# First group's mixer sums, statistics and norm factors placed among the last scan steps

## The reference

```python
# mixer (Mamba), 256 channels x 16 states, scanned over time
def step(h, inp):
    a, b, c = inp
    h = a * h + b
    y = (h * c[:, None, :]).sum(-1)
    return (h, y)
y = ys.transpose(1, 0, 2) + xm * Dp
y = y * silu(z)
x = x + y @ w_out                      # "mixed rows"
h = layernorm(x, ln2_g, ln2_b)         # statistics and factors of the mixed rows
h = gelu(h @ w_ff1 + b_ff1) @ w_ff2 + b_ff2
return x + h                           # and the caller adds this to its own x once more
```

## Time and profile before

| | |
|---|---|
| median of three runs | 940.75 us (940.24 to 942.75) |
| the profiled execution, time | 941.38 us |
| its span in the trace | 939.5 us, 13919 instructions |
| PE busy | 643.7 us (69%) |
| DVE busy | 711.1 us (76%) |
| ACT busy | 538.4 us (57%) |
| POOL busy | 449.6 us (48%) |
| scan instructions `L1232`, 128 of them | 290.5 us busy, 2270 ns each |
| `L1595` matmuls, 1024 of them | 133.6 us busy, 274 ns each |

### The profile page before, as it was taken

How to read it: one execution, slowest core, us unless ns; L and a number is a source line. 1 busy time by engine, 2 the same in 40 slices (tenths; PEclk the granted TensorE clock), 3 DMA queues, 4 the chain that set the end, 5 groups by cost and what they waited for, 6 DMA issues and landing times.

```text
span 939.5 us, 13919 instructions
## 1 busy us (share of the span) xinstructions
PE 643.7 (69%) x4284; PEld 513.3 (55%) x4285; DVE 711.1 (76%) x1785; ACT 538.4 (57%) x1116; POOL 449.6 (48%) x301
## 2 busy tenths in 40 slices
PE   4996116874898767778787887778799971159600
PEld 3775006862343367677676776677677760058600
DVE  6877883446754689999999999999988757845311
ACT  1562002232667989999999999999654620013200
POOL 3000005637400059898989899898710000047474
PEclk9998556996999869999999999999999995559955
DMA  8001101332100123332333233333500002014333
GB/s 203 7 1 53 38 0 43 100 76 54 36 1 6 28 57 104 102 100 101 101 100 104 97 104 95 100 101 101 169 1 1 1 26 64 0 31 109 80 97 81
DMA packets 61778, 62.79 MB, mean 67 GB/s; under 512 B 9079, under 2 KB 42682, under 8 KB 61722
## 3 DMA queue, kind: packets, MB, share of 16 engines
q1 hardware_dynamic: 57178, 52.77, 19.3%
q0 software_dynamic: 4544, 9.32, 4.6%
HBM read 50.40 MB, written 11.67 MB: 66 GB/s over the span
## 4 chain that ended last, share of the span: by engine, by line
DVE 31%; ACT 26%; PE 21%; POOL 11%; issue 8%; DMA 3%; DVEq 0%; POOLq 0%; SPq 0%; ACTq 0%
ACT work L775 12%; DVE work L1232 12%; POOL work L567 6%; POOL r_zs L572 5%; ACT wfold L747 4%; DVE work L985 4%; ACT dBuT L747 4%; PE bank L1678 3%; DMA work<-normed_rows,source 2%; PE bank L1666 1%; PE decay_ps L1666 1%; PE bank L1457 1%; PE decay_ps L1468 1%; PE decay_ps L1625 1%; PE decay_ps L1546 1%
## 5 line engine op out<-in xcount | busy, mean ns | idle before, releaser
L1232 DVE TENSOR_TENSOR_SCAN work<-work,decay_ps 128x1024 f32<-128x1024 f32 x128 | 290.5, 2270 | 1.9 <-PE decay_ps L1582 1.9
L583 POOL TENSOR_TENSOR work<-work,C_bc 128x1024 f32<-128x1024 f32 x86 | 204.5, 2378 | 110.2 <-DVE work L1232 109.7
L567 POOL DMA_INDIRECT work<-normed_rows,source x78 | 74.9, 961 | 297.0 <-DVE source L1085 271.9
L775 ACT ACTIVATE work<-r_delta,Aneg 128x510 f32<-128x510 f32 x256 | 170.1, 712 | 9.0 <-DVE work L1232 7.5
L1595 PE MATMUL bank<-ident,work 128*128 128x128 f32 x1024 | 133.6, 274 | 0.1
L1595 PEld LDWEIGHTS bank<-ident,work 128*128 128x128 f32 x1024 | 116.7, 142 | 0.3 <-POOL work L583 0.3
L583 POOL TENSOR_TENSOR work<-work,win_s 128x1024 f32<-128x1024 f32 x42 | 99.9, 2378 | 11.0 <-DVE work L1232 11.0
L1582 PE MATMUL decay_ps<-ident,wfold 128*128 128x128 f32 x512 | 70.5, 282 | 37.4 <-DVE wfold L1224 24.5
L1582 PE MATMUL decay_ps<-ident,dBuT 128*128 128x128 f32 x512 | 69.5, 280 | 34.5 <-DVE dBuT L1224 34.5
L1582 PEld LDWEIGHTS decay_ps<-ident,wfold 128*128 128x128 f32 x512 | 56.8, 144 | 50.1 <-ACT wfold L747 41.7
L747 ACT ACTIVATE wfold<-duT,B_T 128x256 f32<-128x256 f32 x192 | 82.8, 494 | 1.4 <-PE decay_ps L1582 1.4
(11 more groups left out here) (262 smaller groups left out, 1268.6 us busy)
## 6 DMA issues: line engine op xcount, KB each, us to landing
C_bc<-routed_out SPq DMA_DIRECT2D x86, 256.0 KB, 3.1
win_s<-routed_out SPq DMA_DIRECT2D x42, 256.0 KB, 3.1
routed_out<-work SPq DMA_DIRECT2D x26, 192.0 KB
normed_rows<-r_zs SPq DMA_DIRECT2D x2, 2048.0 KB, 9.4
X<-in_L_attn_a_input_data SPq DMA_DIRECT2D x4, 512.0 KB, 5.7
r_du<-in_L_ffn_W SPq DMA_DIRECT2D x2, 1024.0 KB, 6.7
r_du<-in_L_ffn_W SPq DMA_DIRECT2D x4, 512.0 KB, 8.3
out<-X SPq DMA_DIRECT2D x8, 256.0 KB, 2.4
```

Of the source, the lines that this page charges most:

```text
L567: pool.indirect_dma_start(out=xin[:, i % 2, s, :], out_offset=None, in_=normed_rows, in_offset=bass.IndirectOffsetOnAxis(ap=source[:, k:k ...
L583: pool.tensor_tensor(h[:, m % 4], h[:, m % 4], col(C_bc[m % 3]).broadcast_to([P, NB, G]), ALU.mult).then_inc(c_hC, 1)
L775: last = A(o, d, ACT.Exp, scale=Aneg[:, b, n:n + 1])
L1232: V.tensor_tensor_scan(h[:, m % 4].rearrange("p b t -> p (b t)"), decay[:, m % 2].rearrange("p b t -> p (b t)"), decay_ps[:, m % 2].rearra ...
```

## The change

- out_proj(0) moves to PE's step m = 112 of the scan loop and writes bank 3 instead of bank 4; y_of(6, 0), the next user of bank 3, waits for p_xa of group 0.
- DVE computes XA of group 0 behind scan(113), its statistics behind scan(114), and the 18 factor instructions in scan steps 115 to 122: two links a step, one directly behind the scan and one behind scaled_last (and gated); the first link holds three instructions. The last one is followed by a wait for its own end and the increment of d_factors.
- X is no longer updated by four instructions a group from PSUM (`L1268`), but by one that adds XA over all four tiles (`twice_mixed`). The set-up of `gate` as 1 + rs goes.
- DVE after the loop: mixed(1), twice_mixed(0), factors_of(1), gated(7, 0), mixed(2), factors_of(2), gated(7, 1), finished(0), as before from there.
- PE after turned_dBu(127): summed(124), summed(125), out_proj(1), mixed_turned(0), summed(126), hidden(0) chunks 0 and 1, summed(127), chunks 2 and 3, out_proj(2), y_of(7, 0), mixed_turned(1), dense_out(0), y_of(7, 1), out_proj(3), hidden(1), ... Chunk 3 of group 0 goes to bank 2 instead of bank 1 and waits for chunk 0's gelu.
- ACT after the table load: mixed_rows(0) (waits for scan 126), mixed_turned(0), gelu of chunks 0 and 1, turned_y(7), gelu of chunks 2 and 3, mixed_rows(1), mixed_turned(1), mixed_rows(2), ...

```diff
+def hidden_bank(g, c):
+    return HIDDEN_BANK[0 if g == 0 and c == FFC - 1 else c]
 def slot(i, kind):
...
 GATES = (4, 6)
+FIRST_LINK = STEPS - N + 3
+LAST_LINK = 15
 FIRST = 1
...
     act.preload_act_table(ACT.Gelu_apprx_tanh)
-    act.wait_ge(c_dBu, STEPS)
-    turned_y(NG - 1)
     f = ffn[1]
...
         for c in range(FFC):
+            if g == 0 and c == 0:
+                act.wait_ge(c_y, STEPS - 1)
+            if g == 0 and c == 2:
+                act.wait_ge(c_dBu, STEPS)
+                turned_y(NG - 1)
             act.wait_ge(d_h_ps, g * FFC + (c + 1))
-            A(hT[:, c], bank[HIDDEN_BANK[c]], ACT.Gelu_apprx_tanh, bias=bff1_s[:, c:c + 1]).then_inc(d_h, 1)
+            A(hT[:, c], bank[hidden_bank(g, c)], ACT.Gelu_apprx_tanh, bias=bff1_s[:, c:c + 1]).then_inc(d_h, 1)
...
+    act.wait_ge(c_h, STEPS - 1)
     mixed_rows(0)
     mixed_turned(0)
-    mixed_rows(1)
     for g in range(NG):
         hidden(g)
+        if g == 0:
+            mixed_rows(1)
         if g >= BEHIND:
...
+    def mixed_rows(g):
+        dve.wait_ge(p_out_ps, g + 1)
+        for q in range(GT):
+            j = g * GT + q
+            last = V.scalar_tensor_tensor(out=XA[:, j, :], in0=X[:, j, :], scalar=rs[:, j:j + 1],
+                                          in1=bank[3 if g == 0 else OUT_BANK][:, q * P:(q + 1) * P],
+                                          op0=ALU.mult, op1=ALU.add)
+        last.then_inc(p_xa, 1)
+    def mixed_stats(g):
+        dve.wait_ge(p_xa, g + 1)
+        for q in range(GT):
+            ch.step(V.bn_stats(stats[:, slot(g, 0) + q, :], XA[:, g * GT + q, :]))
+    def twice_mixed(g):
+        at = slice(g * GT, (g + 1) * GT)
+        ch.step(V.tensor_tensor(X[:, at, :], X[:, at, :], XA[:, at, :], ALU.add))
+    def first_factors(k):
+        at = slice(slot(0, 0), slot(0, 0) + GT)
+        st, mean, var, v, t = stats[:, at, :], mean2[:, at], var4[:, at], vv[:, 0, at], t32[:, 0, at]
+        r, o = rs2[:, at], nmr2[:, at]
+        if k > LAST_LINK:
+            return
+        ch.wait()
+        if k == 0:
+            ch.step(V.tensor_tensor(mean, st[:, :, 1], st[:, :, 4], ALU.add))
+            ch.step(V.tensor_tensor(var, st[:, :, 1], st[:, :, 4], ALU.subtract))
+            ch.step(V.tensor_tensor(t, st[:, :, 2], st[:, :, 5], ALU.add))
+        elif k == 1:
+            ch.step(V.tensor_tensor(var, var, var, ALU.mult))
+        elif k == 2:
+            ch.step(V.scalar_tensor_tensor(out=var, in0=t, scalar=4.0 / D, in1=var, op0=ALU.mult, op1=ALU.add))
+        elif k == 3:
+            ch.step(V.tensor_scalar(v, var, 0.25, EPS, ALU.mult, ALU.add))
+        elif k == 4:
+            ch.step(V.tensor_scalar(r.bitcast(I32), v.bitcast(I32), 1, None, ALU.logical_shift_right))
+        elif k == 5:
+            ch.step(V.tensor_scalar(r.bitcast(I32), r.bitcast(I32), -1.0, float(0x5f3759df), ALU.mult, ALU.add))
+        elif k == LAST_LINK:
+            ch.link(V.scalar_tensor_tensor(out=o, in0=mean, scalar=-0.5, in1=r, op0=ALU.mult, op1=ALU.mult))
+            dve.sem_inc(d_factors, 1)
+        elif k % 3 == 0:
+            ch.step(V.scalar_tensor_tensor(out=t, in0=r, scalar=-0.5, in1=r, op0=ALU.mult, op1=ALU.mult))
+        elif k % 3 == 1:
+            ch.step(V.tensor_tensor(t, t, v, ALU.mult))
+        else:
+            ch.step(V.scalar_tensor_tensor(out=r, in0=t, scalar=1.5, in1=r, op0=ALU.add, op1=ALU.mult))
     def gated(g, b):
...
-    ch.step(V.tensor_scalar(gate[:, :], rs, 1.0, None, ALU.add))
     soft(NG - 1)
...
         scan(m)
+        if m == FIRST_LINK - 2:
+            mixed_rows(0)
+        if m == FIRST_LINK - 1:
+            mixed_stats(0)
+        if m >= FIRST_LINK:
+            first_factors(2 * (m - FIRST_LINK))
         if m + 2 < STEPS:
...
             gated(g - 1, GATES.index(n))
+        if m >= FIRST_LINK:
+            first_factors(2 * (m - FIRST_LINK) + 1)
...
-        dve.wait_ge(p_out_ps, g + 1)
-        for q in range(GT):
-            j = g * GT + q
-            ch.step(V.scalar_tensor_tensor(out=XA[:, j, :], in0=X[:, j, :], scalar=rs[:, j:j + 1],
-                                           in1=bank[OUT_BANK][:, q * P:(q + 1) * P], op0=ALU.mult,
-                                           op1=ALU.add))
-        for q in range(GT):
-            j = g * GT + q
-            last = V.scalar_tensor_tensor(out=X[:, j, :], in0=X[:, j, :], scalar=gate[:, j:j + 1],
-                                          in1=bank[OUT_BANK][:, q * P:(q + 1) * P], op0=ALU.mult,
-                                          op1=ALU.add)
-        last.then_inc(p_xa, 1)
-        ch.wait()
-        for q in range(GT):
-            ch.step(V.bn_stats(stats[:, slot(g, 0) + q, :], XA[:, g * GT + q, :]))
+        mixed_rows(g)
+        mixed_stats(g)
+        twice_mixed(g)
...
         dve.wait_ge(d_y_ps, g + 1)
-        dve.wait_ge(p_xa, g + 1)
         for q in range(GT):
...
-    mixed(0)
-    factors_of(0)
     mixed(1)
+    twice_mixed(0)
+    factors_of(1)
     gated(NG - 1, 0)
-    factors_of(1)
     mixed(2)
...
         pe_.wait_ge(c_yT, g + 1)
-        if b == 0:
+        if g == NG - 2 and b == 0:
+            pe_.wait_ge(p_xa, 1)
+        elif b == 0:
             pe_.wait_ge(c_uT, (GT - 1) * min(g + 2, NG))
...
         pe_.wait_ge(c_gated, NB * (g + 1))
-        if g > 0:
+        if g > 1:
             pe_.wait_ge(p_xa, g)
+        elif g == 1:
+            pe_.wait_ge(c_h, STEPS - 1)
         else:
-            pe_.wait_ge(c_h, STEPS - 1)
+            pe_.wait_ge(c_uT, NG * (GT - 1))
         if g > BEHIND + 1:
...
             for b in range(NB):
-                last = mm(bank[OUT_BANK][:, q * P:(q + 1) * P], xm[:, b, j * P:(j + 1) * P], wout_s[:, b, :],
+                last = mm(bank[3 if g == 0 else OUT_BANK][:, q * P:(q + 1) * P],
+                          xm[:, b, j * P:(j + 1) * P], wout_s[:, b, :],
                           start=(b == 0), stop=(b == NB - 1))
...
     turned_du(0, GT - 1)
-    for m in range(STEPS + SUM_LAG):
+    for m in range(STEPS + 1):
         g, n = m // N, m % N
...
             turned_dBu(m)
+        if m == FIRST_LINK - 3:
+            out_proj(0)
         if g + 1 < NG and n in DU_TURNS:
...
             y_of(g - 1, Y_TURNS.index(n))
-        if m == STEPS or m == STEPS + 1:
-            out_proj(m - STEPS)
     def mixed_turned(g):
...
         for c in range(FFC):
-            mm(bank[HIDDEN_BANK[c]], wff1_s[:, c * P:(c + 1) * P], xsT_d, start=True,
+            if g == 0 and c == 1:
+                pe_.wait_ge(c_h, STEPS)
+            if g == 0 and c == 2:
+                summed(STEPS - 1)
+            if g == 0 and c == FFC - 1:
+                pe_.wait_ge(d_h, 1)
+            mm(bank[hidden_bank(g, c)], wff1_s[:, c * P:(c + 1) * P], xsT_d, start=True,
                stop=True).then_inc(d_h_ps, 1)
...
-    y_of(NG - 1, 0)
+    out_proj(1)
     mixed_turned(0)
+    summed(STEPS - 2)
     pe_.wait_ge(s_ff, 32)
-    pe_.wait_ge(c_h, STEPS)
     for g in range(NG):
-        if g + 2 < NG:
+        if 0 < g < NG - 2:
             out_proj(g + 2)
         hidden(g)
+        if g == 0:
+            out_proj(2)
+            y_of(NG - 1, 0)
         if g >= BEHIND:
...
             tokens_turned(g - (BEHIND - 1))
+        dense_out(g)
         if g == 0:
             y_of(NG - 1, 1)
-            pe_.wait_ge(c_gated, NB * (NG - 1) + 1)
-        dense_out(g)
         if g == 1:
...
     logits(NG - 3)
```

## The result

The changed kernel takes 953.62 us (median of 4, 952.5 to 954.2) against 941.12 for the kernel before on the same chip: a ratio of 1.0124, 95% interval 1.0106 to 1.0142. It is 12.5 us slower; the forecast was 938.1. The profiled execution took 953.08 us, its span is 951.1 us (939.5 before).

A forecast was written before the change was run, and what follows sets the result against it. DVE was taken to bound the kernel up to scan 127, no engine in the seam, PE after it. 3.52 us added to the loop less 6.07 saved gave -2.55, so 938.1 us, range 936.6 to 941.2.

The forecast's parts named there:

- the price of a link: Scan loop on DVE: 0.08 us for each of 17 links, 1.36, plus 0.33 for the last; together 1.69 us.
- The sign that was named beforehand: A scan loop longer by over 5 us, or dense_out(0) later than 11 us after scan 127, would refute the forecast.
- The upper bound: Scan loop on DVE: a link behind a scan costs at most 0.33 us, as one with its end waited for.
- the rule on the drain: DVE: next operation starts only once the pipe is empty, so 17 links cost full records; total 939.7 us.
- Sums and statistics: Scan loop on DVE: four XA sums cost 1.04 us, also beside POOL, and four bn_stats 0.79 us.
- out_proj(0) at step 112: Scan loop on PE: 1.79 us fits with 0.3 us to spare before scan 113; costed at nothing.
- The seam: From the scan loop's end to the dense stage: dense_out(1) starts 6.07 us earlier, 5.2 to 6.3 as range.
- mixed_turned(1) was feared to be late: Seam: DVE's factors of group 1 give ACT's rows at 681.48; PE wants them at 682.07, 0.6 us of slack.
- The second: Rival, scan loop: a small instruction behind a scan costs its whole record, 2.9 instead of 1.36; 939.7 us, chance 0.13.
- third: Rival, seam: PE is not packed, mixed_turned(1) waits for DVE and PE loses 1 us; 939.2 us, chance 0.12.
- The fourth: Rival, scan loop: every link stalls DVE, 17 x 0.33 = 5.6 us, net +1.7; 942.4 us, chance 0.05.

The follow-up runs named there:

- e2: Kernel before plus eight 4-column DVE instructions without waits in each of scan groups 2 to 5, operands in SBUF or PSUM; 968.08 us, one run.
- e1: Changed kernel, but in scan steps 115 to 122 POOL multiplies 4 columns instead of 1024; 939.7 us, ratio 0.9976 to the kernel before.
- e5: Changed kernel, but all 18 factor instructions chained behind scaled_last of step 115; 943.67 us, ratio 1.0017 to the kernel before.
- e6: Changed kernel, but each step's second link also directly behind the scan, in front of scaled_last; 957.79 us, ratio 1.0167 to the kernel before.
- e3: Changed kernel with one link a step, directly behind scans 106 to 121, and out_proj(0) at step 104; 939.12 us, ratio 0.9980 to the kernel before.
- e8: Kernel with one link behind each of sixteen scans, its last link raising d_factors without waiting for its own end; 938.6 us, ratio 0.9968 to the kernel before.
- e4: Changed kernel, but group 0's 18 factor instructions chained behind scan 127, none in the loop; 945.71 us, ratio 1.0047 to the kernel before.

## Why the prediction was wrong

**The step that failed** is the price of a link: "For a link behind a scan the trace has no row", with bounds of 0.06 and 0.33 and 0.08 taken, "because a whole scan (2.18 ...) or a scaled_last (0.39 ...) lies between". The wait of a link for the one before was the only cost considered. The eight places directly behind a scan cost 0.05 to 0.08 for each instruction, as taken. The eight behind scaled_last took 15.1 us together (1.42 to 2.33 from their start to the next instruction, the last with its own end waited for) where 0.9 was forecast. The 14.2 between the two, with the 0.44 of PE's lower clock, are the 14.6 by which the loop missed, to within 0.1. The sign that was named beforehand, a loop longer by over 5 us, came with 18.2.

The upper bound was too low because both rows behind it were read at the wrong place. The pair at 676.22 and the last link at 679.34 lie behind 675.14, when POOL had finished its last product. In the loop POOL multiplies for 2.38 of every 2.57 us. The prediction did hold the sums against POOL, and their price was right, but they read one operand from PSUM, as do all DVE instructions of the old loop: the scan, scaled_last and gated have `decay_ps` or `bank` among their inputs. The statistics and the links were the first in the loop to read nothing but SBUF. The statistics (bn_stats) are not held up, as e2 shows; the links are. That they read otherwise than all that had run beside POOL is visible in the `out<-in` column and was what the trace could say; what it costs, it could not. e1, e2, e5 and e6 show the cause. e3 shows that the rest of the forecast held: with every link behind a scan the kernel is 2.4 us faster than before, where 2.55 was forecast.

The Trainium skill states this rule ("SBUF — State Buffer", section "SBUF: two separate sides"): a DVE instruction in a 2-port mode, or one with two SBUF inputs beside a GpSimd instruction that reads SBUF, and the GpSimd instruction exclude each other; the one that starts first keeps the other out for its whole length. The runs agree for two SBUF inputs, 2.17 against 0.14 in e2, and with DVE as the one that waits. They agree for tensor_scalar from SBUF too (2.18), if that ran in a 2-port mode, which no run shows. The page was not weighed in the prediction, and should have been.

Of the rule on the drain, which was weighed, the prediction left out a sentence that the Trainium skill has in the same place ("VectorE: DVE Perf Modes", section "The DRAIN you can't avoid"): "A next op that is not held starts earlier". The runs agree: small instructions that do not wait for POOL let the next one start after 0.05 to 0.08 of their 0.13 to 0.19, behind a scan and, in e1, behind scaled_last alike.

**Point by point.** Sums and statistics: 1.02 and 0.76 for the 1.04 and 0.79 forecast. out_proj(0) at step 112 delayed no scan. The seam: 5.70 less in the changed kernel, 6.18 at full clock (e1, e3), for 6.07; the rest to the end unchanged to within 0.12. Where mixed_turned(1) was feared to be late, PE went on without a pause (699.28 to 700.25 in the changed kernel's timeline), and twice_mixed took 0.67 of record, 0.60 of room.

**The rivals.** The second and third fell: no small instruction costs its record, and PE was packed. The fourth had the right side and the right place, "every link stalls DVE", but the wrong mechanism and price: 0.33 on each of 17, where it was 1.9 on eight and nothing on the others. I gave it 0.05 and an end at 942.4.

## What to carry to other kernels

Before an instruction is put among others on DVE, look at what POOL does at that moment and from where the instruction reads: a price from a stretch where POOL is idle does not hold beside it. Here four columns cost up to a whole product of POOL's, once per product; between two products, or with an operand in PSUM, they were nearly free. The two fastest kernels here, e8 and e3, are those that put one link a step between two products and none beside one. If a stall shows as busy time, compare the recorded duration with that of the same form elsewhere.

## What the runs showed of the hardware

- A DVE instruction that waits for POOL is recorded as busy, not idle: 2.17 us in place of 0.13 for the same instruction (e2). The end of each of the eight waiting links in the changed kernel falls on the end of POOL's instruction to within 0.05 us (648.94 against 648.90).
- The room between two products, where a link is free, is 0.1 to 0.2 us; a link 0.16 behind the first missed it (e6). Three with no wait between them, 0.05 to 0.08 apart, made it in the changed kernel: the third starts at 641.83, POOL's product at 641.87.
- Idle time on PE came back as a lower clock: after 6.77 us of idleness eight transposes took 1.91 instead of 1.04, at a granted clock of 0.50 (e4).
